# A retention block with a mixture of experts: order of the beginning, of the bias's copy, of the residual, form of the last slot, and the engine of x's high part

## What is computed

```
x = x + retention(layernorm(x))
    q, k, v = x @ W_q.T, x @ W_k.T, x @ W_v.T        16 heads of 16
    y = ((q k^T) * decay / 4) v ; normalise y per head and batch; @ W_o.T
x = x + moe(layernorm(x))
    shared = (silu(x @ sw1 + sb1) * (x @ sw3 + sb3)) @ sw2 + sb2
    two of eight experts per token, chosen by the token's number:
    gelu(x @ w1[e] + b1[e]) @ w2[e] + b2[e], mean of the two
    (shared + experts) / 2
```

## Time and profile before

| | |
|---|---|
| profiled execution | 437.39 us |
| its span | 435.6 us |
| median of three runs | 437.23 us |
| TensorE busy | 427.2 us (98%), 6270 matmuls |
| VectorE busy | 328.6 us (75%) |
| ScalarE busy | 216.6 us (50%) |
| GpSimd busy | 74.5 us (17%) |
| granted TensorE clock | 1.0 |

### The profile page before, as it was taken

One profiled execution on the slowest core, in us unless ns is written; L12 is line 12 of the kernel. 1 busy time (PEld: TensorE's weight loads), 2 busy tenths in 40 slices (PEclk: granted clock), 3 DMA queues, 4 the chain that ended last, 5 costly groups with the idle time before them and its releaser, 6 DMA issues.

```text
span 435.6 us, 14430 instructions
## 1 busy us (share of the span) xinstructions
PE 427.2 (98%) x6270; PEld 385.4 (88%) x6270; DVE 328.6 (75%) x789; ACT 216.6 (50%) x416; POOL 74.5 (17%) x69
## 2 busy tenths in 40 slices
PE   6999999999999999999999999999999999999996
PEld 5899999999999999998989988899888999888995
DVE  6887778766878768976798887978879878746423
ACT  3466656546763567535337335473344734346430
POOL 1103223522145013550520000100001000000000
PEclk9999999999999999999999999999999999999999
DMA  7443332232331121325520015100142001120011
GB/s 268 146 147 100 101 102 75 76 84 78 122 116 52 52 99 53 99 100 164 176 96 2 1 50 198 43 0 1 48 155 86 0 0 49 48 96 2 0 50 48
DMA packets 15384, 34.66 MB, mean 80 GB/s; under 512 B 2368, under 2 KB 2656, under 8 KB 14816
## 3 DMA queue, kind: packets, MB, share of 16 engines
q1 hardware_dynamic: 14896, 33.05, 22.8%
q10 hardware_dynamic: 432, 0.79, 0.6%
HBM read 25.44 MB, written 8.40 MB: 78 GB/s over the span
## 4 chain that ended last, share of the span: by engine, by line
PE 90%; DVE 3%; ACT 3%; DMA 2%; issue 1%; ACTq 0%; POOL 0%; DVEq 0%
PE bank L371 50%; PE bank L380 14%; PE bank L381 7%; PE bank L450 6%; PE bank L493 4%; PE bank L480 3%; PE bank L464 3%; DMA wqkv_raw<-wattn 2%; PE bank L429 1%; PE bank L390 1%; ACT vexp L688 1%; ACT kexp L688 1%; PE bank L511 1%; DVE pm L885 1%; PE bank L574 0%
## 5 line engine op out<-in xcount | busy, mean ns | idle before, releaser
L371 PE MATMUL bank<-x2hi,sw_hi 128*128 128x512 f32 x128 | 51.3, 400 | 0.0
L371 PE MATMUL bank<-x2lo,sw_hi 128*128 128x512 f32 x128 | 50.4, 394 | 0.0
L371 PE MATMUL bank<-x2hi,sw_lo 128*128 128x512 f32 x128 | 50.3, 393 | 0.0
L703 ACT ACTIVATE keo<-kT,msk 128x512 f32<-128x512 f32 x32 | 21.4, 715 | 51.8 <-DVE kT L874 51.8
L380 PE MATMUL bank<-w_both,ehi 128*128 128x512 f32 x128 | 46.4, 397 | 0.0
L380 PE MATMUL bank<-sw_both,ghi 128*128 128x512 f32 x128 | 46.3, 394 | 0.0
L775 ACT ACTIVATE sil<-bank,s1b 128x512 f32<-128x512 f32 x32 | 22.0, 688 | 46.6 <-PE bank L371 46.6
L1049 DVE STREAM_TRANSPOSE x2t<-xl 32x256 f32<-32x256 f32 x96 | 41.8, 436 | 1.8
L885 DVE TENSOR_TENSOR pm<-bank,msk 128x512 f32<-128x512 f32 x64 | 39.5, 678 | 2.5 <-PE bank L450 2.5
L371 PE MATMUL bank<-xhi,wqkv_hi 128*128 128x256 f32 x128 | 38.2, 298 | 1.3 <-DVE xlo L869 1.2
L794 ACT ACTIVATE ehi<-xres 128x512 fp32r<-128x512 f32 x32 | 20.2, 633 | 32.9 <-PE bank L381 32.4
(11 more groups left out here) (124 smaller groups left out, 1103.9 us busy)
## 6 DMA issues: line engine op xcount, KB each, us to landing
xin<-xa SPq DMA_DIRECT2D x16, 256.0 KB, 2.9
w_raw<-w SPq DMA_DIRECT2D x16, 256.0 KB, 3.3
xres<-xs SPq DMA_DIRECT2D x16, 256.0 KB, 3.3
x_scratch<-xres SPq DMA_DIRECT2D x16, 256.0 KB, 3.0
xl<-x_scratch SPq DMA_DIRECT2D x8, 512.0 KB, 4.3
xr<-x_scratch SPq DMA_DIRECT2D x4, 1024.0 KB, 4.8
out<-xr SPq DMA_DIRECT2D x7, 512.0 KB, 2.6
sw_raw<-sw SPq DMA_DIRECT2D x6, 256.0 KB, 3.8
```

The source lines that it names most:

```text
L371: mm = nc.tensor.matmul(o, w[c][l], x[c][r], start=first and c == 0 and j == 0, stop=last and c == n - 1 and j == 2)
L703: cp = nc.scalar.activation(keo[:, :, :, odd, :], kT[:].rearrange("p g (c j) -> p c g j", c=CPS), ACT.Copy, scale=parity[:, odd:odd + 1])
```

## The change

1. The first piece of x comes in two halves, token tile 0 on SP's queue and tile 1 on ScalarE's. The identity comes alone, the rest of the masks later. On ScalarE's queue K's weights now stand second, behind that half, and V's third; Q's weights move from there to the third place on SP's queue. The decay comes in two halves, K's first.
2. The first piece goes tile by tile: two transposes each into a bank of its own (`x0_bank`), high part, low part. K's projection still waits for both. One warm-up matmul fewer stands behind the transposes. VectorE takes the low part of K's weights, then the two `xlo`, then the low part of Q's, the sums of piece 1, V's, and K's decay ahead of `ln_apply(1)`.
3. ScalarE makes `xhi` for pieces 0 and 1 only (piece 1 behind `kexp`); from piece 2 on VectorE makes it, directly ahead of `xlo`.
4. `copy_bias` stands behind `high_y`.
5. The residual stands ahead of `ln2_apply` in step 14.
6. The last slot of the last batch is a `split_product` of 24 matmuls of 256 columns, and VectorE adds one half.

```diff
-WARM_UP = (5, 2)
+WARM_UP = (5, 1)
...
+        x0_bank = (b_bank, y_bank)
...
-            load_x(0)
-            sp.dma_start(msk[:], masks).then_inc(msk_landed, 16)
+            sp.dma_start(xin[0][:, 0, :], xa[0, :, 0, :]).then_inc(x_landed[0], 16)
+            sp.dma_start(ident, masks[:, slice(*MASK_COLS["ident"])]).then_inc(ident_landed, 16)
+            sp.dma_start(wqkv_split.raw[:, 0], wattn[:, 0]).then_inc(w_landed[0], 16)
             load_x(1)
-            sp.dma_start(dec[:], decay).then_inc(dec_landed, 16)
+            sp.dma_start(dec[:, 1], decay[:, 1]).then_inc(deck_landed, 16)
+            sp.dma_start(msk[:, P:MASK_W], masks[:, P:MASK_W]).then_inc(msk_landed, 16)
+            sp.dma_start(dec[:, 0], decay[:, 0]).then_inc(decq_landed, 16)
...
+                if isinstance(b, int) and s == NE - 1:
+                    split_product(o_bank[s % 2][:, 0:D], g, [(x[:, 0, :], x[:, 1, :]) for x in w]).then_inc(slot_done, 1)
+                else:
+                    wide_product(o_bank[s % 2][:], g, w).then_inc(slot_done, 1)
...
-            pe.wait_ge(msk_landed, 16)
-            transpose_x(0)
+            pe.wait_ge(ident_landed, 16)
+            for t in range(TILES):
+                pe.wait_ge(xn_ready, t + 1)
+                for c in range(CB):
+                    mm = nc.tensor.transpose(x0_bank[t][:, c * P:(c + 1) * P], xin[0][:, t, c * P:(c + 1) * P], ident)
+                mm.then_inc(t_done, 1)
...
+                high_y(h)
                 if b and s == 1:
                     copy_bias(b - 1, p_bank[1])
-                high_y(h)
                 if h + 1 < PARTS:
                     copy_k(h + 1)
                     copy_v(h + 1)
-                if h + 2 < PARTS:
-                    high_x(h + 2)
...
-            for i in (1, 0, 2):
+            act.dma_start(xin[0][:, 1, :], xa[0, :, 1, :]).then_inc(x0_landed, 16)
+            for i in (1, 2):
                 act.dma_start(wqkv_split.raw[:, i], wattn[:, i]).then_inc(w_landed[i], 16)
             for i in (1, 0, 2):
...
-                if i == 0:
-                    high_x(0)
+                if i == 1:
+                    for t in range(TILES):
+                        act.wait_ge(t_done, t + 1)
+                        nc.scalar.activation(xhi[:, :, t * P:(t + 1) * P], x0_bank[t][:, 0:CB * P].rearrange("p (c t) -> p c t", c=CB),
+                                             ACT.Copy).then_inc(xhi_ready, 1)
             act.wait_ge(msk_landed, 16)
             spread_k(0)
-            high_x(1)
             act.wait_ge(kexp_cleared, 1)
             copy_k(0)
+            high_x(1)
...
+            def high_x(h):
+
+                dve.wait_ge(t_done, h + 2)
+                nc.vector.tensor_copy(xhi[:].rearrange("p c t -> p (c t)"), b_bank[:]).then_inc(xhi_ready, 1)
...
-                else:
-                    ln2_apply(0, h + 3 - PARTS)
                 if b and s >= 2:
                     for j in range(2 * (s - 2), 2 * (s - 2) + 2):
                         residual(b - 1, j, p_bank[j])
+                if h + 3 >= PARTS:
+                    ln2_apply(0, h + 3 - PARTS)
                 if h + 2 < PARTS:
+                    high_x(h + 2)
                     low_x(h + 2)
...
+                if isinstance(b, int) and b == last and s == NE - 1:
+                    nc.vector.tensor_tensor(xr[:, s, :], o_bank[s % 2][:, 0:D], xr[:, s, :], ALU.add).then_inc(o_ready, 1)
+                    return
```

More of the change, by code:

```diff
@@ L185, in moe_retention @@
         w_landed = [sem(f"w{n}_landed") for n in "qkvo"]
-        dec_landed, msk_landed, gn_landed = sem("dec_landed"), sem("msk_landed"), sem("gn_landed")
+        x0_landed, ident_landed = sem("x0_landed"), sem("ident_landed")
+        deck_landed, decq_landed = sem("deck_landed"), sem("decq_landed")
+        msk_landed, gn_landed = sem("msk_landed"), sem("gn_landed")
         xres_landed = [sem(f"xres{j}_landed") for j in range(4)]
@@ L235, in load_x @@
                 if h >= NSUP:
-                    sp.wait_ge(t_done, h - NSUP + 1)
+                    sp.wait_ge(t_done, h - NSUP + 2)
                 sp.dma_start(xin[h % NSUP][:], xa[h]).then_inc(x_landed[h % NSUP], 16)
@@ L325, in step @@
                 if h + 3 <= PARTS:
-                    sp.wait_ge(t_done, h + 3)
+                    sp.wait_ge(t_done, h + 4)
                 if h + 6 < PARTS:
@@ L384, in transpose_x @@
             def transpose_x(h):
-                pe.wait_ge(xn_ready, h + 1)
-                if h:
-                    pe.wait_ge(qT_ready, h)
+                pe.wait_ge(xn_ready, h + 2)
+                pe.wait_ge(qT_ready, h)
                 for c in range(CB):
@@ L411, in project_k @@
             def project_k(h):
-                pe.wait_ge(xlo_ready, h + 1)
+                pe.wait_ge(xlo_ready, h + 2)
                 if h == 0:
@@ L619, in slot @@
                     w += [w2_split.both[:, e::NE, m, :] for m in range(MR)]
-                wide_product(o_bank[s % 2][:], g, w).then_inc(slot_done, 1)
+                if isinstance(b, int) and s == NE - 1:
+                    split_product(o_bank[s % 2][:, 0:D], g, [(x[:, 0, :], x[:, 1, :]) for x in w]).then_inc(slot_done, 1)
+                else:
+                    wide_product(o_bank[s % 2][:], g, w).then_inc(slot_done, 1)
             def experts(b):
@@ L678, in high_x @@
             def high_x(h):
-                act.wait_ge(t_done, h + 1)
+                act.wait_ge(t_done, h + 2)
                 nc.scalar.activation(xhi[:].rearrange("p c t -> p (c t)"), b_bank[:], ACT.Copy).then_inc(xhi_ready, 1)
@@ L851, in ln_sums, with ln_rest @@
                     st = nc.vector.bn_stats(ln_st[:, t, :], x[:, t, :])
+                ln_rest(h, st)
+            def ln_rest(h, st):
                 st.then_inc(ln_stats, 1)
@@ L864, in ln_apply @@
                     ts = nc.vector.tensor_scalar(x[:, t, :], x[:, t, :], ln_mv[:, t, 0:1], ln_r[:, t:t + 1], ALU.subtract, ALU.mult)
-                ts.then_inc(xn_ready, 1)
+                    if h == 0 or t == TILES - 1:
+                        ts.then_inc(xn_ready, 1)
+            def high_x(h):
+                dve.wait_ge(t_done, h + 2)
+                nc.vector.tensor_copy(xhi[:].rearrange("p c t -> p (c t)"), b_bank[:]).then_inc(xhi_ready, 1)
             def low_x(h):
-                dve.wait_ge(xhi_ready, h + 1)
+                dve.wait_ge(xhi_ready, h + 2)
                 nc.vector.tensor_tensor(xlo[:].rearrange("p c t -> p (c t)"), b_bank[:],
@@ L1141, in _ @@
                 nc.vector.memset(vexp[i][:], 0.0).then_inc(v_cleared, 1)
-            ln_sums(0)
+            for t in range(TILES):
+                dve.wait_ge((x_landed[0], x0_landed)[t], 16)
+                st = nc.vector.bn_stats(ln_st[:, t, :], xin[0][:, t, :])
+            ln_rest(0, st)
             ln_apply(0)
@@ L1150, in _ @@
             low_w(0)
+            for t in range(TILES):
+                dve.wait_ge(xhi_ready, t + 1)
+                at = slice(t * P, (t + 1) * P)
+                nc.vector.tensor_tensor(xlo[:, :, at], x0_bank[t][:, 0:CB * P].rearrange("p (c t) -> p c t", c=CB),
+                                        xhi[:, :, at].bitcast(F32), ALU.subtract).then_inc(xlo_ready, 1)
             low_w(1)
-            low_x(0)
+            ln_sums(1)
             low_w(2)
-            ln_sums(1)
+            dve.wait_ge(deck_landed, 16)
+            decay_k(0)
             ln_apply(1)
+            dve.wait_ge(decq_landed, 16)
+            decay_q(0)
             dve.wait_ge(msk_landed, 16)
-            dve.wait_ge(dec_landed, 16)
-            decay_k(0)
-            decay_q(0)
             ln_sums(2)
@@ L1245, in step @@
                 elif h + 3 < PARTS:
-                    pool.wait_ge(xn_ready, h + 4)
+                    pool.wait_ge(xn_ready, h + 5)
                 elif h + 1 < PARTS:
```

## The result

Six runs of the kernel after took 433.56 to 434.81 us, median 434.09; six of the kernel before 436.67 to 437.95, median 437.14. The ratio is 0.9931 with a 95% interval from 0.9918 to 0.9944: 3 us faster, against a forecast of 434.0. The profiled execution took 434.14, span 432.34, against 437.39 and 435.57 (435.6 as rounded ahead of the prediction).

The account below looks back on a forecast made before the run. TensorE, busy 98% of the span, bounds the kernel, so only its gaps, beginning and end can be won. Gains 1.35 + 1.12 + 0.33 + 0.39 = 3.19 us; 437.39 - 3.19 = 434.2, as median 434.0; range 433.2 to 435.8.

Parts of the forecast that it names:

- First product at 8.3: Beginning: TensorE's first product starts at 8.3 us instead of 9.35, with K's weights on the path.
- So I take 6.1: Beginning: K's weights, behind 128 KB on their queue, come at 6.1 us, between bounds of 4.9 and 7.2.
- the transposes cost the path nothing; they hide behind the weights: Beginning: transposes of piece 0 add 0; were the weights early, x's chain would end only 0.4 us sooner.
- early-weights rival: Beginning: K's weights come at 4.9, x's chain sets the first product at 7.95, 433.7 us; chance 0.14.
- The rule weighed: Beginning's loads: the skill's 2.0 us plus bytes over 436 GB/s gives x 2.6, K's weights near 4.2; rows preferred.
- K's projection of piece 1 at 16.2, `xlo` as the new wait: Beginning: it starts 7.9 us behind the first product, at 16.2 instead of 17.59, waiting for `xlo`; gain 1.35 us.
- The cast takes 0.68: Steps: each `xhi` cast on VectorE takes 0.68 us, bounds 0.60 and 1.4, and fits beside its 8.1 busy of 10.36.
- Gain: 4 x 0.28 = 1.12: Steps 6, 9, 10 and 14: `xhi` on VectorE removes 0.28 us lost before K's projection in each, 1.12 us.
- Nothing on TensorE waits for them in that window: 0: Three steps: bias's copy behind `yhi` ends ScalarE's copies 0.4 us sooner, but gains TensorE 0.
- Residual 0.33: Scores of piece 15: residual ahead of `ln2_apply` starts them 0.12 instead of 0.45 behind the last V matmul, 0.33 us.
- Last slot 0.39: End: 24 matmuls lose 0.07 us on TensorE, one VectorE instruction less gains 0.46; gain 0.39 us.
- the slower rival: Beginning: clock falls from 2.4 to 1.2 GHz, piece 0's 36 matmuls take up to 4.3 us more, 438.3; chance 0.04.

Follow-up runs that it names:

- e1: Kernel before with all of the change but its beginning (bias's copy, cast on VectorE, residual, last slot): 435.94 us, ratio 0.9949.
- e2: Kernel before with only the bias's copy moved behind y's high part: one run, 436.06 us.
- e3: Kernel before with only the cast of x's high part from piece 2 on moved to VectorE: one run, 437.46 us.
- e4: Kernel after with x's high part from piece 2 on back on ScalarE, behind V's copies: one run, 433.79 us.
- e5: Kernel after with VectorE also making the high part of piece 1: 434.08 us, ratio 0.9913 to the kernel before.
- e8: Kernel after with no warm-up matmuls at all: one run, 436.64 us.
- e11: Kernel after, unchanged, as measure for the runs beside it: 434.39 us, ratio 0.9924 to the kernel before.
- e7: Kernel after with VectorE making piece 1's high part and eight instead of ten zero matmuls ahead of the transposes: 434.05 us, ratio 0.9918.
- e12: The kernel of e5 measured again, later: 433.81 us, ratio 0.9910 to the kernel before.
- e13: Kernel after with the last slot as before (512- and 256-column matmuls, VectorE adds both halves): one run, 435.26 us.
- e14: The kernel of e4 again, timed with six runs: 434.87 us, ratio 0.9944 to the kernel before.
- e6: Kernel after with eight instead of ten zero matmuls ahead of the transposes: 434.16 us, ratio 0.9916 to the kernel before.

## Why the prediction was right, point by point

The time came out within 0.1 us, and part of that is luck. The terms 1.35, 1.12, 0.33 and 0.39 measured 1.34, 1.12, 0.24 and 0.49: the last two errors cancel, the first two terms came out by paths that were not the forecast's. The profile of before could also have shown another beginning: with the same beginning the first product stands at 9.35 there and at 10.03, 9.81 and 10.11 in e1, e2 and e3, K's projection of piece 1 at 17.59, 17.70, 17.49 and 18.42.

*First product at 8.3: it came at 8.19, but by another path.* Two steps failed and offset each other. "So I take 6.1" for K's weights: they were used at 5.30, not far from the lower bound of 4.9, so the half of x ahead on their queue cost 0.4 in this pair and not 1.2 (over all traces they are used at 4.91 to 5.33 with the old order of the loads and at 5.05 to 5.81 with the new one). And "the transposes cost the path nothing; they hide behind the weights" did not hold: the transposes waited for the ten zero matmuls, and the first of them still ran at the lower level of the clock (0.21 us to the next one's start, then 0.14 and 0.11). The early-weights rival nearly got its condition, and not its 7.95; e4, where the level rose sooner, came to 7.79. The forecast's timeline of TensorE had left out the warm-up because before it always ended ahead of the normalised x (transposes at 7.31).

*The rule weighed.* The two halves of x, 128 KB each on two queues at once, landed 2.6 and 2.8 us after issue. The Trainium skill (DMA: Bandwidth & Descriptors, Anatomy of one DMA) would give 2.3 by its fit for one transfer, an estimate. It gives the fit for DMAs that GpSimd issues, which the prediction did not say, while these come from SP and ScalarE; they took 0.3 and 0.5 longer. K's weights near 4.2, as the prediction worked them out from it, were too early by 1.1, and the 6.1 too late by 0.8.

*K's projection of piece 1 at 16.2, `xlo` as the new wait: right,* 16.25 and 0.66. From the first product to it lay 8.06 and not 7.9. e1, with the old order there, needs 17.70 - 10.03 = 7.67, so moving `high_x(1)` behind `kexp` costs 0.39 of what the earlier first product gives, and against e5, where the projection waits for nobody, 0.73.

*The cast takes 0.68: right* (688 ns each over 14), and it fits into VectorE. The row by lines of after:

```profile
L891 DVE CAST xhi<-bank 128x512 fp32r<-128x512 f32 x14 | 9.6, 688 | 7.1 <-PE bank L397 7.1
```

*"Gain: 4 x 0.28 = 1.12": the traces differ by that, but for other reasons.* One of the four was no wait for `xlo`; in step 9 TensorE waited for its instructions (last section), which happened in the profile of before and not in that of after. That this 0.28 went is no merit of either part. The other three, 0.84, are real. The line of waits read "1.2, 4, 0.5"; with the first product's 0.55 taken off, three times 0.22 are left, and the fourth place should have been looked at by itself.

*"Nothing on TensorE waits for them in that window: 0" for the bias's copy failed.* ScalarE's four copies of K, four of V and `xhi` stood behind it in a chain without slack, and K's projection at its end. Against the state sums the chain came 0.32 sooner in e2 (`xlo` 0.06 behind their start instead of 0.38), just over the 0.28 that was missing. Each of the two parts alone removes the three stalls (e2, e3), so neither's worth adds to the other's: of the sum's 1.12 the bias's copy could have had 0.84, and the cast only what is left.

*Residual 0.33: it was 0.24.* The floor was mis-sized: I took 0.12, the distance between products; between the last product and the scores it is 0.21 with nothing late. In e3, whose residual still stands behind `ln2_apply`, the scores came 1.70 behind the start of the last V group, against 1.84 before and 1.60 in after: the wait depends on how early VectorE is.

*Last slot 0.39: it was 0.43 to 0.49.* TensorE loses 0.03 instead of 0.07, and 0.46 to 0.52 go behind the last matmul; VectorE's 0.46 was right, the rest lies in the store, whose end comes 2.29 to 2.35 us behind the last add.

*The clock.* The granted clock reads 1.00 in every stretch, which was the forecast's evidence against the slower rival, and it was no evidence (below). The case's 0.04 was still fair for one matmul less.

## What to carry to other kernels

When two parts of a change shorten the same chain, price each alone before the sum: here a reordering of two instructions did what moving 14 casts to another engine was given credit for. A time that comes out right is no proof of its path; look in the new trace for each step of it, what was late and what was not. And count stalls by what ended each one, not by equal distances: four gaps of 0.28 us had two causes. Where no engine ended one, count TensorE's instructions up to it and look at the loads of instructions in the trace.

## What the runs showed of the hardware

**The granted clock and the pace of matmuls disagree at the start.** Zero matmuls of 256 columns start 0.43 us apart and later 0.21, products 0.21 in e8 and at the start of e3 and 0.12 elsewhere: the levels of 1.2 and 2.4 GHz. The row says 1.00 throughout, in after from 2 us on:

```profile
3.00:4.00 1.00, 1.00 (x4) 0.82 (x3) 0.63 (x3) 0.42 (x1) 0.00 (x0) 1.00 1.04 246
```

Four zero matmuls touch this microsecond; at the 0.21 us that they reach later it would be five or six. The Trainium skill (TensorE: Matmul & The Clock Gate, Seeing it yourself) warns that such clock events can be unreliable; here the pace is the better witness. The level rose during the zero matmuls in before and e4, in e11 only behind the transposes, with the same work ahead of it from 1.98 us on, and in e3, whose beginning is that of before, only within the first products (0.21 us apart up to 11.6 us). The page says too that the moment of the rise varies from run to run (What's actually happening), which agrees. Between e4 and e11, whose beginning is the same, the first product moves by 0.6 us (7.79 to 8.40).

**TensorE can run out of instructions.** Groups of short matmuls (13 ns apart) sometimes lose 0.1 to 0.45 us: 0.28 us in the profile of before, 0.55 in e3, 0.44 to 0.74 in e5, e7 and e12, 0.51 in e13, 0.5 in e14 and 0.2 in e8, none above 0.1 in after, e1, e2, e4, e6 and e11. No engine ends these breaks, and at 30 to 32 us of e5 no bytes moved at all. The packed traces show what they are. Counted over weight loads and matmuls together, the main break stands behind 193 instructions and a multiple of 256 more: 22 x 256 in before, 33 and 34 x 256 in e3, 4, 5 and 6 x 256 in e5 and e12, 4 and 5 x 256 in e7 and e13, 11 x 256 in e8, 3, 10 and 33 x 256 in e14, though the warm-ups differ. And the page of after lists a queue of instructions:

```profile
q8 instruction: 44, 0.72, 0.7%
```

These are 44 loads of 16 KB, 64 bytes for each of 256 instructions. The k-th such load belongs to the boundary at 193 + k x 256: at each of the first 42 boundaries in all 14 traces, TensorE starts the instruction behind it no sooner than 1.21 us after that load has ended, and at all the breaks named it is 1.2 to 1.6 us. So TensorE waited there for its next 256 instructions. In before, the load ended at 117.78 and the state sums of step 9 went on at 118.99; in e3, 177.59 and 179.17. With matmuls 13 ns apart, each with its weight load, 256 instructions last 128 x 13 ns = 1.7 us, with products 0.12 us apart 15 us; all the breaks but one (e14 at 28.05, in K's projection) stand in the short groups. What makes a load late isn't shown. The breaks are as large as the single terms of this change, and in a single profile they look like part of it.
